# Cross-attention block: the preparation stage in a new explicit order on every engine

## The reference

```python
xq  = layer_norm(x, qn_w, qn_b)
ctx = layer_norm(context, cn_w, cn_b)
q = (xq @ q_w).reshape(B, N, H, D)
kv = (ctx @ kv_w).reshape(B, M, 2, H, D)
k, v = kv[:, :, 0], kv[:, :, 1]
attn = einsum('bnhd,bmhd->bhnm', q, k) * D ** -0.5
attn = softmax(where(xa_mask[:, None], -max, attn))
x = x + einsum('bhnm,bmhd->bnhd', attn, v).reshape(B, N, C) @ proj_w + proj_b
h = layer_norm(x, n2_w, n2_b)
out = x + gelu(h @ fc1_w + fc1_b) @ fc2_w + fc2_b
```

## Time and profile before

| what | us |
|---|---|
| median of 3 runs (lowest to highest) | 1134.07 (1132.53 to 1134.37) |
| the profiled execution, its own time | 1134.04 |
| its span | 1132.3 |
| PE busy | 1105.1 (98%) |
| DVE busy | 581.7 (51%) |
| ACT busy | 401.8 (35%) |
| POOL busy | 231.6 (20%) |
| loop entered (first score of the first loop step on PE) | 54.7 |
| first score of the second and the third step | 79.0 and 101.8 |

### The profile page before, as it was taken

The page is one execution under the profiler, slowest core; times in us unless marked ns, Lnnn a source line. Parts: engine busy times, 40 slices in busy tenths (PEclk is TensorE's granted clock), DMA queues, the critical chain, the costliest instruction groups (busy, mean ns, idle before and its releaser), DMA issues.

```text
span 1132.3 us, 16382 instructions
## 1 busy us (share of the span) xinstructions
PE 1105.1 (98%) x5849; PEld 942.3 (83%) x5849; DVE 581.7 (51%) x1154; ACT 401.8 (35%) x1158; POOL 231.6 (20%) x186
## 2 busy tenths in 40 slices
PE   4999999999999999999999999999999999999998
PEld 4789989999999788888888888888888888888887
DVE  7888878887888856532423323322332332232212
ACT  3456655665666634411211311221221131121110
POOL 2343355335544421100100100100110110010000
PEclk9999999999999999999999999999999999999999
DMA  7011111131110034201002002002002001100101
GB/s 246 8 37 57 38 38 56 57 121 38 58 58 20 29 120 132 66 23 61 1 1 75 1 2 75 1 1 75 1 1 74 2 1 38 38 1 1 38 1 38
DMA packets 40144, 48.76 MB, mean 43 GB/s; under 512 B 10965, under 2 KB 19197, under 8 KB 40087
## 3 DMA queue, kind: packets, MB, share of 16 engines
q1 hardware_dynamic: 37919, 43.74, 11.8%
q10 hardware_dynamic: 2168, 4.21, 1.0%
HBM read 30.54 MB, written 16.78 MB: 42 GB/s over the span
## 4 chain that ended last, share of the span: by engine, by line
PE 79%; DVE 16%; ACT 2%; issue 2%; DVEq 0%; POOL 0%; ACTq 0%; POOLq 0%
PE bank L1308 31%; PE bank L1279 31%; PE bank L1195 8%; PE bank L1153 3%; PE bank L1134 2%; DVE nmax L840 2%; DVE PTl L863 2%; DVE bnst L886 2%; DVE xTl L846 1%; DVE S L833 1%; DVE xhat L898 1%; PE bank L1291 1%; DVE qTl L852 1%; ACT S L642 1%; DVE aTl L868 1%
## 5 line engine op out<-in xcount | busy, mean ns | idle before, releaser
L1308 PE MATMUL bank<-w,gTh 128*128 128x512 f32 x1024 | 319.2, 393 | 0.0
L1054 DVE CAST gTh<-g 128x512 fp32r<-128x512 f32 x128 | 56.9, 445 | 443.8 <-ACT g L744 443.8
L744 ACT ACTIVATE g<-bank,cols 128x512 f32<-128x512 f32 x128 | 88.0, 688 | 472.6 <-PE bank L1279 471.5
L1308 PEld LDWEIGHTS bank<-w,gTh 128*128 128x128 f32 x1024 | 192.4, 188 | 42.7
L1308 PE MATMUL bank<-w,gTl 128*128 128x512 f32 x512 | 200.4, 391 | 0.0
L1279 PE MATMUL bank<-hT0h,w 128*128 128x512 f32 x512 | 162.2, 398 | 0.4 <-DVE w L1011 0.4
L1279 PE MATMUL bank<-hT1h,w 128*128 128x512 f32 x512 | 159.2, 392 | 0.1
L480 POOL TENSOR_TENSOR hrs<-hve,mhalf 128x1 f32<-128x1 f32 x32 | 17.6, 549 | 551.7 <-DVE hve L1028 551.7
L1308 PEld LDWEIGHTS bank<-w,gTl 128*128 128x128 f32 x512 | 96.1, 188 | 22.0
L1279 PEld LDWEIGHTS bank<-hT0h,w 128*128 128x128 f32 x512 | 94.7, 188 | 22.1 <-DVE w L1011 0.6
L1279 PEld LDWEIGHTS bank<-hT1h,w 128*128 128x128 f32 x512 | 95.1, 188 | 20.2 <-issue 0.9
(11 more groups left out here) (103 smaller groups left out, 1794.6 us busy)
## 6 DMA issues: line engine op xcount, KB each, us to landing
xr<-in_x SPq DMA_DIRECT2D x16, 512.0 KB, 3.5
x_scratch<-xr SPq DMA_DIRECT2D x16, 512.0 KB, 2.8
x<-x_scratch SPq DMA_DIRECT2D x8, 1024.0 KB, 5.6
out<-x SPq DMA_DIRECT2D x7, 1024.0 KB, 4.3
w1raw<-in_L_xattn_fc_w SPq DMA_DIRECT2D x16, 256.0 KB, 3.0
w2raw<-in_L_xattn_fc_w SPq DMA_DIRECT2D x16, 256.0 KB, 2.7
kvw<-in_L_xattn_kv_w ACTq DMA_DIRECT2D x2, 1024.0 KB, 11.4
qraw<-in_L_xattn_q_w ACTq DMA_DIRECT2D x1, 1024.0 KB, 11.8
```

The costliest lines, as they stand in the source:

```text
L744: act.activation(g[:, :], bF[j % 2][:, :], ACT.Gelu, bias=cols[:, F1B + j:F1B + j + 1]).then_inc(a_gelu.sem, 1)
L1054: dve.tensor_copy(gT[HI][j % 4][:, :], g[:, :]).then_inc(v_ghi.sem, 1)
L1308: mm = pe.matmul(bC[t][:, :], gT[d][j % 4][:, t * P:(t + 1) * P], w2[:, j, w, :], start=(j == 0 and i == 0), stop=(j == JT - 1 and i == 2))
```

## The change

It touches the preparation alone; the loop, the last steps and the MLP issue what they issued. All that stood ahead of the steps is now in step -3 (`prep="rows"`) and step -2, each prep step is a list of its own that ends with `return`, and the code shared with the loop loses its special cases.

- SP: x of unit 0 comes first, and the context behind the three rows; x of units 1, 2, 3 wait in addition for the keys weight, the values weight, and the projection weight.
- ACT issues q_w ahead of the others and in four pieces of 128 rows, each with its own semaphore.
- Order of PE: rows, x_T of unit 0, context transposes, q_bias (into bank 7 instead of 2), q(0), q(1), keys, q(2), q(3), values(0); then scores, x_T, the queries of unit 1, values(1), and at the very end the wait for `wpl` (before: ahead of the scores).
- Tile 0 of unit 0 goes the way of tile 1: POOL subtracts, ACT takes one whole exponential, DVE sums.
- POOL clears `vbd` after unit 1's rstd.
- DVE makes `wpl` last of all.

```diff
@@ pipeline
-        step(static(-3), norm=True)
+        step(static(-3), norm=True, prep="rows")
@@ sync_program
-        sp.dma_start(cx[0:M, :, :], ctx.rearrange("b m c -> m b c")).then_inc(d_ctx, 16)
+        load_x(static(0))
         for i in range(3):
             load_row(sp, i)
+        sp.dma_start(cx[0:M, :, :], ctx.rearrange("b m c -> m b c")).then_inc(d_ctx, 16)
         load_mask(static(0))
         load_mask(static(1))
-        load_x(static(0))
+        sp.wait_ge(d_kw, 16)
+        load_x(static(1))
+        sp.wait_ge(d_vw, 16)
+        sp.wait_ge(d_x[0], 16)
+        load_x(static(2))
         sp.dma_start(projb[:, :], proj_b.rearrange("(a c) -> a c", a=1).to_broadcast([P, C])).then_inc(d_projb, 16)
-        sp.wait_ge(d_x[0], 16)
-        load_x(static(1))
-        load_x(static(2))
+        sp.wait_ge(d_pw, 16)
         sp.wait_ge(d_x[1], 16)
         load_x(static(3))
@@ gpsimd_program, step
+            if prep == "q":
+                may_negate(k.plus(2))
+                negative(k.plus(2))
+                x_rstd()
+                for b in range(B):
+                    pool.memset(f32(vbd[:, b, :, :, :]).rearrange("p a b c -> p (a b c)"), 0.0).then_inc(p_zero, 1)
+                return
+            if prep == "scores":
+                v_max.wait(pool, k.plus(1), 0)
+                less_max(0).then_inc(p_less0, 1)
+                v_max.wait(pool, k.plus(1), 1)
+                less_max(1).then_inc(p_less.sem, 1)
+                may_negate(k.plus(2))
+                negative(k.plus(2))
+                probs(0)
+                x_rstd()
+                probs(1)
+                pool.wait_ge(d_projb, 16)
+                return
@@ scalar_program
+        for kk in range(KT):
+            act.dma_start(qraw[:, kk, :], q_w.rearrange("(k p) n -> k p n", p=P)[kk]).then_inc(d_qk[kk], 16)
         act.dma_start(kvw[:, :, 0:C], kv_w[:, 0:C].rearrange("(k p) n -> p k n", p=P)).then_inc(d_kw, 16)
-        act.dma_start(qraw[:, :, :], q_w.rearrange("(k p) n -> p k n", p=P)).then_inc(d_qw, 16)
@@ scalar_program, step
+            if prep == "q":
+                act.wait_ge(v_wscale, 1)
+                wq_hi(0)
+                wq_hi(1)
+                x_hi(0)
+                x_hi(1)
+                wq_hi(2)
+                wq_hi(3)
+                ctxT_half()
+                act.wait_ge(v_qbias, 1)
+                q_hi(0)
+                keys_hi()
+                q_hi(1)
+                values_hi(0)
+                act.wait_ge(d_pw, 16)
+                act.activation(wp[HI][:, :, :], praw[:, :, :], ACT.Copy).then_inc(a_wp, 1)
+                return
+            if prep == "scores":
+                x_hi(0)
+                x_hi(1)
+                exp_all0()
+                exp_all(1)
+                t_scores.wait(act, s, UT * KT - 1)
+                q_hi(0)
+                q_hi(1)
+                values_hi(1)
+                return
@@ tensor_program, step
             if prep == "q":
-                keys()
                 x_T(0)
                 x_T(1)
+                ctx_T()
                 q_bias()
-                pe.wait_ge(v_wq, 1)
-            elif prep == "scores":
-                x_T(0)
-                x_T(1)
+                pe.wait_ge(v_wq, KT)
+                q(0)
+                q(1)
+                keys()
+                q(2)
+                q(3)
+                values(0)
+                return
+            if prep == "scores":
                 pe.wait_ge(v_keys, 1)
-                pe.wait_ge(v_wp, KT)
                 for t in range(UT):
                     for g_ in range(KT):
                         score(t, g_)
-                values(0)
+                x_T(0)
+                x_T(1)
+                for m in range(KT):
+                    q(m)
+                values(1)
+                pe.wait_ge(v_wp, KT)
+                return
```

More of the change, by code:

```diff
@@ L201, in sem @@
         return nc.alloc_semaphore(name)
-    d_rows, d_ctx, d_kw, d_vw, d_qw, d_pw, d_projb = (sem(f"d_{n}") for n in
-                                                      ("rows", "ctx", "kw", "vw", "qw", "pw", "projb"))
+    d_rows, d_ctx, d_kw, d_vw, d_pw, d_projb = (sem(f"d_{n}") for n in ("rows", "ctx", "kw", "vw", "pw", "projb"))
     d_vbd = [sem("d_vbd0"), sem("d_vbd1")]
@@ L510, in step @@
                 add_projb(1)
[L511 to L515, removed]
             if norm2 is not None:
                 h_rstd(static(0), norm2)
-            if norm and prep is None:
+            if norm:
                 x_rstd()
             if scores:
[L522 to L526, removed]
+                v_max.wait(pool, k.plus(1), 1)
+                less_max(1).then_inc(p_less.sem, 1)
             if norm2 is not None:
                 h_bias(static(0), norm2)
-            if norm and prep is not None:
-                x_rstd()
             if scores:
-                n = k.plus(1)
                 for t in range(UT):
[L534 to L539, removed]
+                    probs(t)
         def h_rstd(n, t):
@@ L906, in residual @@
                 dve.tensor_tensor(v, bV[t][:, :].unsqueeze(1), v, ALU.add).then_inc(v_res.sem, 1)
-            if prep == "q":
-                q_weights()
+            if prep == "rows":
+                stats()
+                columns()
+                v_bn.wait(dve, n, UT - 1)
+                variance()
+                ctx_stats()
+                normed()
+                ctx_variance()
+                return
+            if prep == "q":
+                wq_lo(0)
+                wq_lo(1)
+                x_lo(0)
+                x_lo(1)
+                ctx_normed()
+                wq_lo(2)
+                wq_lo(3)
+                q_bias()
+                ctxT_half()
+                zero_keys(LO)
+                stats()
+                v_bn.wait(dve, n, UT - 1)
+                variance()
+                q_lo(0)
+                keys_lo()
+                q_lo(1)
+                normed()
+                values_lo(0)
+                return
+            if prep == "scores":
+                for g_ in range(KT):
+                    masked(0, g_)
+                maximum(0)
+                for g_ in range(KT):
+                    masked(1, g_)
+                maximum(1)
+                x_lo(0)
+                x_lo(1)
+                sum_of(0).then_inc(v_esum0, 1)
+                recip(0)
+                exp_sum()
+                recip(1)
+                stats()
+                v_bn.wait(dve, n, UT - 1)
+                variance()
+                q_lo(0)
+                q_lo(1)
+                normed()
+                values_lo(1)
+                proj_weights(range(KT))
+                return
             if scores:
@@ L912, in step @@
                 masked(0, 1)
-            if front and prep != "scores":
+            if front:
                 x_lo(0)
@@ L1256, in step @@
                 q(3)
-            if prep == "scores":
-                values(1)
             if back:
```

188 lines of the change are left out of this document (91 added, 97 removed).

## The result

| | before | changed |
|---|---|---|
| median, us (lowest to highest) | 1134.22 (1132.53 to 1134.53) | 1141.12 (1140.68 to 1141.89) |
| profiled execution, own time / span | 1134.04 / 1132.3 | 1140.68 / 1138.9 |
| loop entered (first loop score on PE) | 54.7 | 61.8 |
| next step's first score (the mark) | 79.0 | 86.0 |

What follows compares the result with a forecast made beforehand. It took the loop's entry as what the change moves: entry 60.9 plus one step of 22.8 gives 83.7 against 79.0, so 1134.04 plus 4.7 is 1138.7 us, slower; range 1134.5 to 1142.6.

Steps and rivals of the forecast that it cites:

- the entry's cause: Loop entry: PE waits for wpl, made last on DVE behind vtok; serial tail from 56.9 to an entry at 60.9.
- the front comes out even: Up to the first scores: about 10 us gained at wql goes into q_bias, q(0), q(1) at half clock, and kbdl.
- q_bias at half the clock: q_bias, now ahead of q(0) on PE, runs at 1.2 GHz: about 7.0 us, from 14.4 to 21.4.
- the idle ahead of unit 1's queries: PE idles from 42 to 46.1, then low clock; the 48 query products take 7.1 us instead of 5.6.
- I cost this edit at nothing: One whole exponential replacing sixteen in the middle gains nothing, hidden by PE's 48 query products and values(1).
- One of its own signs: In the changed profile, the granted clock was to stand at 0.50 in q_bias, from about 14.4.
- the second rival: q_bias alone at full clock, rest as forecast: 3.3 us less, 1135.4, no change by its bound; chance 0.15.
- one step of 22.8: From loop entry at 60.9 to the next first score at 83.7: one step, costing 22.8 us.
- One: Clock up from q_bias on: q_bias, q(0), q(1) and unit 1's queries shorter; entry 53.8, 1131.6, faster; chance 0.12.
- Three: Low clock lasts through the keys: 3.9 becomes 7.8, entry 64.8, 1142.6; chance 0.12.
- Four: The early x is not early, landing up to 5.7 us later; with 2 us, 1140.7; chance 0.10.
- The named extra price of wpl beside POOL's additions: Before the loop: wpl meeting POOL's projb additions costs up to 1.3 us more; left to the range.

Runs made afterwards that it cites:

- e4: Changed kernel with tile 0 of unit 0 again in sixteen exponentials, without POOL's subtraction and DVE's sum; 1141.36 us against 1141.12.
- e2: Changed kernel with q_bias moved behind q(0) and q(1) on PE; 1141.02 us against 1141.12.
- e1: Changed kernel with DVE's four wpl moved early, behind the first query parts, and ACT's wph copy ahead of its query-bias wait; 1134.83 us.
- e6: Kernel before with only POOL's two memsets of vbd moved late, behind unit 1's xhat; 1129.23 us, ratio 0.9957.
- e8: Kernel before with only DVE's wpl moved behind the second values and PE's wait for them to the loop's entry; 1138.23 us, ratio 1.0038.
- e11: Changed kernel with POOL's memsets of vbd put back early, directly behind crs; 1144.91 us, ratio 1.0096.
- e3: Changed kernel with values(0) on PE moved back behind the first scores and x_T; 1140.49 us, ratio 1.0055.
- e7: Changed kernel with the edits of e1, e2 and e3 together; 1134.76 us, ratio 1.0006.

## Why the prediction was right, and where a size was off

**Right by its own steps:** the entry's cause, PE waiting for wpl as the last item of DVE; "the front comes out even" (scores at 38.2, forecast 37.2, before 37.5); q_bias at half the clock, 6.91 for 7.0; the context normalisations 0.99 for 1.05; the first query part on ACT at 27.1, 1.1 later than the forecast 26; the idle ahead of unit 1's queries with a low clock behind it (7.48 for 7.1); and "I cost this edit at nothing" for the exponentials, which e4 bears out. One of its own signs did not show: the granted clock reads 1.00 over q_bias, not 0.50. That q_bias and the queries behind it ran at the lower level is read from their length, 6.91 against 3.70 and 0.21 a product against 0.12. What q_bias at full clock would be worth was overrated: the second rival put it at 3.3, e2 made it short and won nothing, because the low clock followed it.

**Mis-sized:** the mark was to come at 83.7 and came at 85.95, 2.25 late; the median is 2.4 over the forecast. The entry is 0.94 of it (forecast 60.9): xTl ends 0.7 late (context and keys, 4.45 in the chain instead of 3.9), the 48 queries are 0.4 longer, and the small terms nearly cancel. The larger term, 1.3, is in "one step of 22.8". The forecast put the low clock behind two idle gaps of PE and left it out behind the third, the 4 us at the entry that it had itself worked out. The first step measured 24.1. e1 shows 23.2 for it without the gap, so 0.9 of the 1.3 goes with the gap and 0.4 is what this step takes over 22.8 at full clock; e4 shows up to 2.1 for the gap. The forecast's own had 24.3 for the first step of the kernel before, at full clock and for another reason: there the two xhat from 54.50 on took 2.62 while POOL was busy with probs and an addition, and PE waited 0.68 for xhat.

**The rivals.** One and two (the clock up at or in q_bias) did not happen: 6.91. Three (low clock through the keys) did not happen in this kernel, where the keys took 4.64, but did in e2, with q_bias directly ahead. Four: x was early (DVE's statistics of it start at 4.08). The transfer that was late was another, the context: issued at 2.31 behind x and the rows, landed at 7.60; DVE idled 1.24 for it. The named extra price of wpl beside POOL's additions was not paid: the additions ended at 58.64, wpl began at 59.01 and took 2.48 for four. The prediction calls the 2.63 of the earlier trace rows the one of its kind beside a POOL operation; the timeline has two more of the sixteen there, with 1.56 at 378.76 and 0.85 at 400.33, so the price varies.

**Where the 6.9 went.** The memsets alone give 4.8 in the old order and 3.8 in the new. wpl last alone costs 4.3 in the old and 6.3 in the new. What the rest of the change costs shows in two pairs of kernels that are alike in both: e6 and e1 (memsets late, wpl early), 1129.23 and 1134.83, and e8 and e11 (memsets early, wpl last), 1138.23 and 1144.91. The rest costs 5.6 in one pair and 6.7 in the other. The three prices do not add up exactly, since each depends on the others. The PE timelines of e6 and then e1, at the context's transposes and at unit 0's first score:

```profile
7.83 1.26 PE L1090 MATMUL bank<-ident,cx 77*128 77x77 f32 x8 [7.83 <-DVE cx L780]
...
32.81 0.38 PE L1136 MATMUL bank<-kbdh,qTh 128*128 128x308 f32 x1
```

```profile
14.34 1.29 PE L1168 MATMUL bank<-ident,cx 77*128 77x77 f32 x8 [2.32 <-DVE cx L829]
...
38.45 0.38 PE L1212 MATMUL bank<-kbdh,qTh 128*128 128x308 f32 x1 [0.45 <-DVE qTl L901]
```

The transposes start 6.5 later in e1, and from there to the first score the new order is 0.9 shorter, 24.1 for 25.0. From the transposes to the mark the two are within 0.6. So in this pair the whole loss stands ahead of the context's transposes. In e8 and e11 they start at 13.03 and 17.58, which is 4.55 of the 6.7. Two things put them there. The context lands late: at 8.24 in e1, where DVE's statistics of it begin at 4.08 in e6; it is issued behind x and the rows. And DVE does two xhat, two wql and two xTl (3.5 in e1's chain) between its statistics and its normalisation. The queries ahead of the keys and q_bias in front, which e2 undoes in part without a gain, cost nothing net by this reading. Of the other parts the exponentials are 0 and the four pieces a gain of at most 1.0. This is read from the traces: no run moved the context's load or those DVE operations alone, so it is not shown by an experiment.

## What to carry to other kernels

When work is moved to the end of a prologue, price the wait it puts on the bottleneck engine with everything queued ahead of it on the engine that does the work, and count the low clock after that idle as well: here 2.5 us of work cost 6.3. Compare also when the first product of a chain can start at all: here the context came to PE 6.5 us later in the new order than in the old one with the memsets moved. A reordering bundles parts of opposite sign, so run each alone: the moved memsets were worth 4.8 us, and this had been invisible under a change that lost. An edit that empties one engine's chain is worth nothing where it hands as much work to the next one in line.

## What the runs showed of the hardware

- **The granted clock column can read 1.00 where products run at half speed.** Two rows of the changed kernel, with the columns of the earlier trace rows:

```profile
22.40:25.60 3.20, 3.20 (x17) 3.20 (x17) 2.74 (x5) 0.00 (x0) 0.00 (x0) 1.00 0.02 5
48.00:51.10 3.10, 3.10 (x17) 3.10 (x16) 2.23 (x5) 1.17 (x1) 2.56 (x2) 0.50 0.16 19
```

  Seventeen query products of one shape in nearly the same time, once under 1.00 and once under 0.50. In this trace the wrong reading stands ahead of the first fall that the profile shows; there the products' own spacing (0.21 or 0.12) tells the level. The forecast's 5.1 for q(0), q(1) came from records at 0.50 and measured 5.33 under a column of 1.00.
- **VectorE beside GpSimd.** A normalisation with one large operand is held up by a memset (4.66 against 0.99), while e1's four wpl, with two operands in SBUF, took 2.48 at 29.3 beside the same memsets and 2.48 at 59.0 without them. The Trainium skill (SBUF — State Buffer, section Who interferes with whom) says that tensor_scalar, among others, can enter a mode that takes the port pair shared with GpSimd and then block on each other, and that two SBUF inputs contend with GpSimd's reads but not with its writes. By that rule the trace agrees on both counts.
- **A transfer's landing varies.** The context took 5.29, 5.49, 5.93, 5.94 and 6.37 us in profiles of the changed kernel, e2, e1, e3 and e7, with the same queue order, and here each of them stands in the chain.
